# Edge-maximum passes of a four-layer graph network: one-hots compared on the chip, step tables in one load, one group more of skew

## What is computed

```python
def _edge_conv(x, src, dst, W1, b1, W2, b2, n_nodes):
    xi = x[dst]
    xj = x[src]
    m = jnp.concatenate([xi, xj - xi], axis=-1)
    h = jax.nn.relu(m @ W1 + b1) @ W2 + b2
    agg = jax.ops.segment_max(h, dst, num_segments=n_nodes)
    return jnp.where(jnp.isfinite(agg), agg, 0.0)
...
x = x + _L3_gnn_ref(h, edge_index, ...)
```

## Time and profile before

| | |
|---|---|
| median of 3 runs | 14299.75 us (14287.04 to 14313.22) |
| profiled execution | 14320.16 us, span 14318.4 us |
| granted TensorE clock, mean of the span | 0.737 of full speed |
| the three calls of `edge_maxima` | about 10210 to 11499, 11598 to 12885, 12985 to 14273 us |

### The profile page before, as it was taken

The page is one execution under the profiler, slowest core; times in us unless marked ns, Lnnn a source line. Parts: engine busy times, 40 slices in busy tenths (PEclk is TensorE's granted clock), DMA queues, the critical chain, the costliest instruction groups (busy, mean ns, idle before and its releaser), DMA issues. The chain is left out here.

```text
span 14318.4 us, 190871 instructions
## 1 busy us (share of the span) xinstructions
PE 8175.9 (57%) x43167; PEld 6995.2 (49%) x43168; DVE 7060.5 (49%) x14119; ACT 2195.9 (15%) x6082; POOL 7386.1 (52%) x7807
## 2 busy tenths in 40 slices
PE   4677344442444436666364455555577767776776
PEld 3666344442344435555243355544466656665665
DVE  4555211113333337888788455566444444444444
ACT  0000000000111110000000000034233323332332
POOL 3666577773566506777000377600266646654665
PEclk6555566665566568988788666666799989998998
DMA  2222555554222215666343244432244434443444
GB/s 72 84 85 84 140 97 97 97 96 106 63 60 59 57 20 171 204 203 198 77 135 102 75 131 130 130 88 81 72 129 129 129 97 129 129 122 103 129 129 115
DMA packets 1058180, 1558.40 MB, mean 109 GB/s; under 512 B 340400, under 2 KB 512092, under 8 KB 1058128
## 3 DMA queue, kind: packets, MB, share of 16 engines
q1 hardware_dynamic: 667296, 920.90, 22.6%
q0 software_dynamic: 329776, 470.23, 14.8%
q10 hardware_dynamic: 61056, 166.75, 3.0%
HBM read 1223.25 MB, written 333.93 MB: 109 GB/s over the span
## 5 line engine op out<-in xcount | busy, mean ns | idle before, releaser
L1438 POOL DMA_INDIRECT T<-gather_d,srci x2496 | 2360.1, 946 | 2563.6 <-PEq L70 1119.2
L1069 PE MATMUL PS<-T 128*128 x3392 | 1132.2, 426 | 1045.8 <-DMA T<-wide_d,slot_idx 340.2
L1551 DVE TENSOR_TENSOR_SCAN T<-T,PS 128x512 f32<-128x512 f32 x624 | 798.7, 1280 | 1798.3 <-PE PS L1480 1746.9
L732 POOL DMA_INDIRECT added_d<-T,slot_idx x840 | 1305.5, 1554 | 364.3 <-issue 194.5
L1069 PEld LDWEIGHTS PS<-T 128*128 128x128 f32 x3392 | 769.2, 259 | 1231.3 <-issue 1174.9
L1480 PE MATMUL PS<-T,W 128*128 128x512 f32 x1248 | 749.6, 684 | 982.5 <-issue 836.7
L1244 PE MATMUL PS<-T 128*128 128x260 f32 (+1 forms) x3360 | 870.1, 421 | 518.2 <-DVE T L1293 316.5
L1031 POOL DMA_INDIRECT T<-wide_d,slot_idx x848 | 940.9, 1110 | 378.4 <-issue 254.5
L1070 PE MATMUL PS<-T,ident 128*128 128x256 f32 (+1 forms) x3392 | 1072.0, 408 | 0.0
L504 POOL DMA_INDIRECT T<-score_d,slot_idx x848 | 856.5, 1010 | 373.6 <-issue 312.1
L1466 PE MATMUL PS<-T 128*128 128x128 f32 x4992 | 1009.2, 285 | 68.7 <-DMA T<-gather_d,srci 64.4
(11 more groups left out here) (249 smaller groups left out, 16224.6 us busy)
## 6 DMA issues: line engine op xcount, KB each, us to landing
T<-onehot_t_d SPq DMA_DIRECT2D x1258, 256.0 KB
T<-step_first_d SPq DMA_DIRECT2D x624, 256.0 KB
edge_rows_d<-T ACTq DMA_DIRECT2D x212, 512.0 KB
T<-step_src_d SPq DMA_DIRECT2D x422, 256.0 KB
T<-edge_rows_d SPq DMA_DIRECT2D x210, 512.0 KB
onehot_t_d<-T SPq DMA_DIRECT2D x212, 256.0 KB
edge_rows_d<-T ACTq DMA_DIRECT2D x212, 256.0 KB
T<-edge_rows_d SPq DMA_DIRECT2D x210, 256.0 KB
```

The source lines that it names most:

```text
L732: gp.indirect_dma_start(added_d[k][:, :], bass.IndirectOffsetOnAxis(ap=slot_idx[:, k:k + 1], axis=0), quad(OUT8, g)[:, u * P:(u + 1) * P], ...
L1069: T_.matmul(spot(g, u), part(quad(OT8, g), u), T2[:, bass.ds(bs[4 * g + u] * width, width)], start=True, stop=False)
L1438: gp.indirect_dma_start(part(R[n % RING], u), None, gather_d[:, :], bass.IndirectOffsetOnAxis(ap=srci[:, k:k + 1], axis=0)).then_inc(rows_ ...
L1551: V.tensor_tensor_scan(SC[i], MK[r], bank(2 + i), SC[1 - i][:, GROUP * P - 1:GROUP * P], ALU.add, ALU.max).then_inc(scanned.h, 1)
```

## The change

- **One-hots.** The load of `OT` goes. VectorE makes `OT` for each group with one comparison (`make_hots`): the place of each edge in its block, broadcast to all partitions, against the partition's own number `pcol`. There are two buffers of `OT` instead of four.
- **Loads.** Places and masks of eight steps (two groups) come in one load of 1 MB from a new table `quads_d`, of which each row holds 512 places and 512 masks. The chip holds two halves of two groups each. SyncE issues the load of groups 2m and 2m+1 when the scan of group 2m-3 is done.
- **Setup.** One more store (`step_place_d`), a wait, and two copies within DRAM that fill `quads_d`.
- **Edges.** The source rows are now transposed into PSUM (one instruction a step instead of a matmul against the identity with two), ahead of the waits for one-hots and A, and A times `OT` is added to them.
- **Skew.** In iteration n TensorE makes turn(n-1), edges(n+1), products(n), ends(n-2); before it was edges(n), turn(n-1), products(n), ends(n-1). ScalarE does relu(n+1) and lay(n+2), VectorE adds the ends of n-2 and makes the one-hots of n+2. The gathers and edges run for one group more than there are; `ST` is cleared once.

```diff
--- before.py
+++ after.py
@@ -161,6 +161,8 @@
         step_dst_d = dram("step_dst_d", [ALL + 2, P])
         step_first_d = dram("step_first_d", [ALL, P])
         step_last_d = dram("step_last_d", [ALL, P])
+        step_place_d = dram("step_place_d", [ALL, P])
+        quads_d = dram("quads_d", [ALL // GROUP, 2 * GROUP * P])
         score_d = dram("score_d", [ROWS, 1])
         gather_d = dram("gather_d", [ROWS, DIM])
         wide_d = dram("wide_d", [ROWS, WIDE])
...
@@ -245,9 +249,13 @@
                     mid = step_dst_d[1:ALL + 1, :]
                     for k, d in ((0, step_src_d), (1, mid), (3, step_first_d), (4, step_last_d)):
                         sp.dma_start(d.rearrange("(c p) e -> p c e", p=P), stepr[:, :, k, :]).then_inc(stored.h, 16)
+                    sp.dma_start(step_place_d.rearrange("(c p) e -> p c e", p=P), far).then_inc(stored.h, 16)
                     sp.dma_start(step_dst_d[0:1, :], W[0:1, 0:P]).then_inc(stored.h, 16)
                     sp.dma_start(step_dst_d[ALL + 1:ALL + 2, :], W[0:1, 0:P]).then_inc(stored.h, 16)
-                    sp.wait_ge(stored.h, 16 * 7)
+                    sp.wait_ge(stored.h, 16 * 8)
+                    for k, d in enumerate((step_place_d, step_first_d)):
+                        sp.dma_start(quads_d[:, k * GROUP * P:(k + 1) * GROUP * P], d.rearrange("(q u) e -> q (u e)", u=GROUP)).then_inc(stored.h, 16)
+                    sp.wait_ge(stored.h, 16 * 10)
                     sp.wait_ge(loaded.h, 16 * 6)
 
                 @block.gpsimd
...
@@ -1419,10 +1427,12 @@
 
         def edge_maxima():
 
-            ring = lambda k: [T2[:, k * 2048 + r * GROUP * P:k * 2048 + (r + 1) * GROUP * P] for r in range(RING)]
-            pair = lambda k: [T2[:, 6144 + k * 1024 + i * GROUP * P:6144 + k * 1024 + (i + 1) * GROUP * P] for i in range(2)]
-            R, OT, MK = (ring(k) for k in range(3))
-            RT, SC, ST, O, AB = (pair(k) for k in range(5))
+            wide = GROUP * P
+            R = [T2[:, r * wide:(r + 1) * wide] for r in range(RING)]
+            places, firsts = ([T2[:, 2048 + g * 2 * wide + k * wide:][:, 0:wide] for g in range(RING)] for k in range(2))
+            halves = [T2[:, 2048 + h * 4 * wide:2048 + (h + 1) * 4 * wide] for h in range(2)]
+            pair = lambda k: [T2[:, 6144 + k * 2 * wide + i * wide:][:, 0:wide] for i in range(2)]
+            RT, SC, ST, O, AB, OT = (pair(k) for k in range(6))
             w2 = wcol(2)
             maxima = T1[:, ROWS:2 * ROWS]
             trips = GROUPS // RING
@@ -1431,7 +1441,7 @@
             with nc.Block() as block:
                 @block.gpsimd
                 def _(gp):
-                    for n in range(GROUPS):
+                    for n in range(GROUPS + 1):
                         gp.wait_ge(edges_made.h, edges_made.done(n - RING))
                         for u in range(GROUP):
                             k = LEAD + n * GROUP + u
@@ -1440,32 +1450,22 @@
 
                 @block.sync
                 def _(sp):
+                    def steps(m, h):
+                        sp.wait_ge(scanned.h, scanned.done(m * 2 - 3))
+                        row = quads_d[bass.ds(m * 2 + LEAD // GROUP, 2), :].rearrange("(a s) e -> a (s e)", a=1)
+                        sp.dma_start(halves[h], row.to_broadcast([P, 4 * wide])).then_inc(steps_in[h].h, 16)
+
                     with sp.Fori(0, trips) as j:
-                        for r in range(RING):
-                            n = j * RING + r
-                            s0 = j * per_trip + (r * GROUP + LEAD)
-                            sp.wait_ge(edges_made.h, edges_made.done(n - RING))
-                            sp.dma_start(OT[r], onehot_t_d[:, bass.ds(j * (per_trip * P) + (r * GROUP + LEAD) * P, GROUP * P)]).then_inc(hots_in[r].h, 16)
-                            sp.wait_ge(scanned.h, scanned.done(n - RING))
-                            row = step_first_d[bass.ds(s0, GROUP), :].rearrange("(a s) e -> a (s e)", a=1)
-                            sp.dma_start(MK[r], row.to_broadcast([P, GROUP * P])).then_inc(firsts_in[r].h, 16)
+                        for h in range(2):
+                            steps(j * 2 + h, h)
+                    steps(2 * trips, 0)
 
                 @block.tensor
                 def _(pe):
                     for s in (edges_made, products_made):
                         s.lead(pe)
-                    for s in (turned, ends_made):
-                        s.lead(pe, 1)
-
-                    def make_edges(n, j, r):
-                        pe.wait_ge(hots_in[r].h, hots_in[r].at(16 * j + 16))
-                        pe.wait_ge(rows_in[r].h, rows_in[r].at(64 * j + 64))
-                        pe.wait_ge(laid.h, laid.done(n))
-                        pe.wait_ge(relued.h, relued.done(n - 2))
-                        for u in range(GROUP):
-                            T_.matmul(part(bank(r % 2), u), part(AB[r % 2], u), part(OT[r], u), start=True, stop=False)
-                            last = T_.matmul(part(bank(r % 2), u), part(R[r], u), ident[:, :], start=False, stop=True)
-                        last.then_inc(edges_made.h, 1)
+                    turned.lead(pe, 1)
+                    ends_made.lead(pe, 2)
 
                     def turn(n, i):
                         pe.wait_ge(scanned.h, scanned.done(n))
@@ -1473,6 +1473,18 @@
                         for u in range(GROUP):
                             last = T_.transpose(part(bank(4 + i), u), part(SC[i], u), ident[:, :])
                         last.then_inc(turned.h, 1)
+
+                    def make_edges(n, j, r):
+                        edges = bank(r % 2)
+                        pe.wait_ge(rows_in[r].h, rows_in[r].at(64 * j + 64))
+                        pe.wait_ge(relued.h, relued.done(n - 2))
+                        for u in range(GROUP):
+                            T_.matmul(part(edges, u), part(R[r], u), ident[:, :], start=u == 0, stop=False, is_transpose=True)
+                        pe.wait_ge(hots_made.h, hots_made.done(n))
+                        pe.wait_ge(laid.h, laid.done(n))
+                        for u in range(GROUP):
+                            last = T_.matmul(part(edges, u), part(AB[r % 2], u), part(OT[r % 2], u), start=False, stop=u == GROUP - 1)
+                        last.then_inc(edges_made.h, 1)
 
                     def make_products(n, i):
                         pe.wait_ge(relued.h, relued.done(n))
@@ -1487,14 +1499,16 @@
                             last = T_.matmul(part(bank(6 + i), u), part(O[i], u), part(ST[i], u), start=True, stop=True)
                         last.then_inc(ends_made.h, 1)
 
+                    make_edges(0, 0, 0)
                     with pe.Fori(0, trips) as j:
                         for r in range(RING):
                             n = j * RING + r
-                            make_edges(n, j, r)
                             turn(n - 1, 1 - r % 2)
+                            make_edges(n + 1, j + (r + 1) // RING, (r + 1) % RING)
                             make_products(n, r % 2)
-                            make_ends(n - 1, 1 - r % 2)
+                            make_ends(n - 2, r % 2)
                     turn(GROUPS - 1, 1)
+                    make_ends(GROUPS - 2, 0)
                     make_ends(GROUPS - 1, 1)
 
                 @block.scalar
@@ -1519,15 +1533,18 @@
                         act.wait_ge(ends_made.h, ends_made.done(n - 2))
                         S_.activation(ST[i], bank(4 + i), ACT.Copy).then_inc(turned_out.h, 1)
 
-                    lay(0, 0, numbers_at(act, brow, LEAD, GROUP, BLOCKS))
+                    first = numbers_at(act, brow, LEAD, 2 * GROUP, BLOCKS)
+                    lay(0, 0, first[0:GROUP])
+                    lay(1, 1, first[GROUP:])
+                    relu(0, 0)
                     with act.Fori(0, trips) as j:
                         for r in range(RING):
                             n = j * RING + r
                             if r % 2 == 0:
-                                bs = numbers_at(act, brow, j * per_trip + (r * GROUP + LEAD + GROUP), 2 * GROUP, BLOCKS)
-                            relu(n, r % 2)
+                                bs = numbers_at(act, brow, j * per_trip + ((r + 2) * GROUP + LEAD), 2 * GROUP, BLOCKS)
                             turn_out(n - 1, 1 - r % 2)
-                            lay(n + 1, 1 - r % 2, bs[r % 2 * GROUP:r % 2 * GROUP + GROUP])
+                            relu(n + 1, 1 - r % 2)
+                            lay(n + 2, r % 2, bs[r % 2 * GROUP:r % 2 * GROUP + GROUP])
                     turn_out(GROUPS - 1, 1)
 
                 @block.vector
@@ -1536,20 +1553,26 @@
                     for i in range(2):
                         V.memset(SC[i], -BIG)
                         V.memset(O[i], 0.0)
+                        V.memset(ST[i], 0.0)
                     V.memset(maxima, 0.0)
                     c.link(V.memset(H[:, :], 0.0))
```

(21 more changed lines are left out.)

22 lines of the change are left out of this document (15 added, 7 removed).

## The result

The changed kernel takes **14,342 us** (median of 20 runs) and the kernel before 14,308 us (20 runs): a ratio of 1.0024, 95% interval [1.0017, 1.0031]. That is slower by a little more than the 0.2% that can be told from no change, and it is almost the figure of the rival that the forecast gave 0.16: the late signal stays whole, 14,350 us.

The account below looks back on a forecast made before the run. It took a loop of waits at 6.12 us a group as the bound, falling to 5.15 under load and gathers: 561 us less in three passes, 8 more in setup, so 14,300 less 553 is 13,747 us; range 13,630 to 14,360.

Parts of the forecast that it names:

- the late signal stays whole: Rival: TensorE's edges signal stays late whatever the order, the group stays at 6.12 us, 14,350 us; chance 0.16.
- What bounds the kernel now: Edge-maximum passes: no engine full, a loop of waits at 6.12 us a group, 4.5 us printed work and 1.6 us unexplained.
- Step (1): Skew in TensorE's order: relu, ScalarE's copy and the table's addition leave the loop; the longest left is 4.2 us.
- Step (4): GpSimd's gathers as the new bound: 1.25 us each, 5.00 us a group.
- Step (5): The 1 MB load for two groups: 6.2 us, plus 4.0 us of work behind it, gives 5.1 us a group.
- Step (3): One-hots compared on VectorE: 0.35 us a group, free unless the group falls below 3.7 us.
- (2): Edges as four transposes take 0.45 us from TensorE, costed at nothing since TensorE is not the bound.
- (6): Starts, ends and setup: 187 us less in each pass, 561 in three; setup adds 8 us.
- Part of it stays: Rival: the 1.6 us belongs to the edges block, loop 5.8 us, 14,155 us; chance 0.22 together with blocked gathers.
- VectorE blocks the gathers: Rival: GpSimd loses each comparison's 0.35 us, group 5.35 us, 13,870 us; chance 0.22 together with partial lateness.
- The late load: Rival: the 1 MB load takes 10.8 us, the group 7.4 us, 15,160 us; chance 0.09.
- The clock falls: Rival: TensorE's clock drops; at 1.2 GHz throughout the loop takes 6.7 us, 14,720 us; chance 0.08.

Follow-up runs that it names:

- x8: The kernel before with only the first of each group's four gathers, on a chip where TensorE's signals come late: 13,207 us, against 14,132 us for the kernel before.
- x12: The kernel before with two gathers a group instead of four, on a chip without late signals: 13,093 us.
- x5: The kernel before, unchanged, profiled on a second chip where TensorE's signals come late: 14,132 us.
- x6: The changed kernel, unchanged, on a second chip where TensorE's signals come late: 14,166 us, ratio 1.0018 to the kernel before.
- x16: The kernel before, unchanged, profiled on a chip without late signals: 13,462 us.
- x2: The changed kernel with four plain loads of 64 KB a group in place of GpSimd's gathers: 13,139 us, against 13,492 us for the kernel before.
- x13: The changed kernel with plain loads of 64 KB instead of gathers, run again on a chip without late signals: 13,142 us.
- x1: The changed kernel with only the first of each group's four gathers: 13,058 us, against 13,492 us for the kernel before.
- x15: The changed kernel, unchanged, on a chip without late signals: 13,457 us against 13,486 us for the kernel before, ratio 0.9978.
- x7: The kernel before with VectorE's comparison and the load of eight steps, without skew and with old edges: 14,124 us, ratio 0.9997 to the kernel before.

## Why the prediction was wrong

The measured time lies inside the range, 13,630 to 14,360, but the likeliest case, 553 us less, did not come: the kernel is 34 us slower.

- **What bounds the kernel now.** The reading was right: a loop of waits with 1.6 us in it, at the full clock, that nothing printed accounts for. Where there is no hold that 1.6 us is not there, and the rest of the loop is the 4.5 us of the sum (4.51 in x8 and x12).
- **Step (1), the step that failed.** It counted on the skew to take the late signal off the loop, since its readers came off it, and so left a loop of 4.2 us. The late signal stayed on the loop: the group took 6.12 us before and after. Nor does the signal lag by a fixed time behind its work: what was 1.6 us in four groups of five is now anything from nothing to over 3 us. On the second such chip it was the same, 6.03 us before (x5) and 6.05 after (x6). That leaving out gathers ends the hold is shown by x8; by what means four gathers bring it about stays open.
- **Step (4).** GpSimd was not a new bound at 5.0 us. Where the signals are on time, it was the old one: 5.13 us a group in x16. The 5.0 us counted every gather at the 1.25 us of a pass's start; the rest is gathers held up by VectorE, 0.15 us a group. The forecast compared a loop without the hold after with a loop with it before. A price of zero for the skew follows from the earlier trace rows and the printed 4.5 us alone: the loop was shorter than the gathers.
- **Step (5).** The load was priced too high: from issue to landing it takes 4.9 us (median, the pages of x2 and x13) or 4.7 (the page of x1), not 6.2. The formula was good: (4.7 + 4.0) / 2 = 4.35 us a group, and x1, with its gathers nearly gone, took 4.37, while VectorE waited for the load 42.3 us in 800. The Trainium skill's "DMA: Bandwidth & Descriptors", section "Bandwidth", has 6.15 us of engine time for 1 MB from HBM; this load, which SyncE issues and which brings the same 8 KB to all partitions, has landed in less than that, and the measurement decides. The latency of 1 to 1.5 us in the lower bound had no row; in x15 the first packet starts 1.0 us after the issue.
- **Step (3).** The comparison takes 0.46 us, not 0.35. VectorE had room for it (x7: no slower), but it is not free for GpSimd, as x15 shows.
- **Steps (2) and (6).** Free edges: right. Where nothing is won, the costs were 50 us by the forecast (a group, a later start, the setup) and 41 in the profile. The later start was 8.5 us a pass against 8. The extra group, 6.1 us a pass by the forecast, cost nothing. The first gather came 15 us later where 8 were reckoned for the setup, but in x5 and x6 it came 3.6 us earlier in the changed kernel, so that part is scatter between executions.

The comparison of the earlier trace rows after the change, x15, first pass:

```profile
L1575 DVE TENSOR_SCALAR T<-T,pcol x210: 458/462/723, 10014.0 to 11069.7; 128x512 f32<-128x512 f32 x105
```

- **Rivals.** *The late signal stays whole* was right in mechanism: the pace of 6.1 us is kept whatever the order. That its 14,350 is so near 14,342 is partly luck, since the extra group cost nothing and the first gather came later than reckoned. Its evidence, was in the text and deserved more than 0.16: a pace that TensorE's clock does not move is not set by TensorE's order. *Part of it stays* (5.8 us) did not come. *VectorE blocks the gathers* was right in mechanism and wrong in size and sign. It was priced at 0.35 us a group on top of gathers that nothing disturbed; but the marks of the kernel before cost the gathers 0.15 us a group already, and with the comparisons it is 0.08 (x16 and x15). On the first chip 395 of 2,508 gathers were lengthened after the change and 3 of 2,496 before, under a pace that the hold set. The Trainium skill's "SBUF — State Buffer", section "SBUF: two separate sides", has VectorE's two-port modes lock GpSimd out of writing descriptors for a whole instruction. The trace agrees, in that a gather ends 0.82 us after the comparison in which it starts; whether the comparison runs in such a mode no run shows. *The late load* did not come: VectorE waited for it 3.0 us in 1,000 us after the change. *The clock falls*: 0.91 after 0.95 between the first and the last scan of the second pass, with the average pace unchanged.

VectorE's and ScalarE's waits after the change on the first chip, 1,000 us of the first pass (us, times, longest):

```profile
ACT T L1534 <- remote: 212.2, 37, 6.6
...
ACT T L1529 <- remote: 88.7, 28, 3.4
...
DVE T L1575 <- DMA T<-quads_d: 3.0, 4, 1.6
```

## What to carry to other kernels

Before reordering a loop, take away the work that you suspect and see what pace is left: one run with a quarter of the gathers (4.51 us against 6.03) says more than the whole sum. Give the floor of each engine to the kernel before as well as to the one after; if both stand on the same floor, a shorter loop is worth nothing. When the mean of an instruction moves, look at its longest ones and at what ran beside them, before explaining the mean by traffic. And if a signal comes later than its work, and at the same pace at either clock, give much weight to the case that a new order is held at that pace too, as here on two chips.

## What was not expected of the hardware

- **The same kernel runs at two paces on different chips.** It takes 14,308 and 14,132 us in two comparisons and 13,475 to 13,492 on four chips. Of the 670 us between x5 and x16, 564 are the three passes (6.03 against 5.12 us a group) and 108 come before them. The sign of this change depends on it: 1.0024 and 1.0018 on the one kind, 0.9978 on the other. No chip was met twice, so a state of the chip at that time is not told apart from the chip itself.
- **A hold is of all TensorE's signals at once.** In the hold shown five come out together within 0.4 us, up to 6 us late, while TensorE's own records run on. VectorE's signal for a comparison came on time in the midst of it.
- **VectorE holds up GpSimd's gathers, and it depends on the instruction.** The gathers that start 0.05 to 0.5 us into the marks (0.69 us long) are all lengthened, 293 of 293 in x16, and end 0.82 us after them. The comparison does the same in x15; the scan doesn't.
- **Records go missing where signals are held.** The trace of the kernel before has 101,438 and 107,228 records of semaphore updates on the holding chips and 200,789 on another, of the same program. In the first trace only 56 of the 627 ends signals of the passes are recorded, though the kernel waits for each. Where x8 has no hold nothing much is missing: 59 records a group, of about 61 (x12's 77.3 less the 16 of its second gather), against 45 of 109 in x5. Whether the recording itself holds the signals is open: every time here comes with a recorded span, and no run was made without. The Trainium skill's "NOTIFIC — the notification-queue block", section "7.1 Overflow: three behaviours, one of which stalls the engine", says that the block which takes such records pushes back on its producers when its own pipeline is full. No run here shows that it does so in this case.
